# ScalarE takes shared results, row numbers and the slot map; TensorE's maps and shared chunks stand in another order; one gather goes in front of scatters

## The reference, cut to what matters

```python
x = L0_attn_x                                    # 8 x 512 tokens, 256 wide
x = layernorm(x + attn(x))                       # gated attention, two layernorms of its own
# the mixture of experts, on all 4096 tokens:
shared = gelu(xf @ Wfc_s + bfc_s) @ Wproj_s + bproj_s          # 256 -> 1024 -> 256
probs  = softmax(xf @ Wr);  topk_p, topk_i = top_k(probs, 2)   # 2 of 8 experts
topk_p = topk_p / sum(topk_p)
for e in range(8):
    h = gelu(xf @ Wfc[e] + bfc[e]) @ Wproj[e] + bproj[e]
    routed = routed + h * gate[:, e:e + 1]       # gate is 0 for experts not chosen
x = layernorm(x + shared + routed)
```

## Time and profile before

| | |
|---|---|
| median of 3 runs | 1000.14 us (999.05 to 1000.84) |
| the profiled execution: time / span | 1000.27 us / 998.4 us |
| PE busy | 936.1 us (94% of the span) |
| DVE busy | 752.9 us (75%) |
| ACT busy | 566.6 us (57%) |
| POOL busy | 234.3 us (23%) |
| mean granted clock of PE | 0.979 |
| chain that ended last | PE 57%, DVE 6%, ACT 1%, DMA 1%, issue 1% (shares below 1% left out) |

### The profile page before, as it was taken

The page is one execution under the profiler, slowest core; times in us unless marked ns, Lnnn a source line. Parts: engine busy times, 40 slices in busy tenths (PEclk is TensorE's granted clock), DMA queues, the critical chain, the costliest instruction groups (busy, mean ns, idle before and its releaser), DMA issues.

```text
span 998.4 us, 17975 instructions
## 1 busy us (share of the span) xinstructions
PE 936.1 (94%) x5998; PEld 830.3 (83%) x5998; DVE 752.9 (75%) x1823; ACT 566.6 (57%) x1008; POOL 234.3 (23%) x170
## 2 busy tenths in 40 slices
PE   4979999999997988899999999999999989999995
PEld 3767788788876777799999999999999989999994
DVE  5799889888876589677777777777777879984846
ACT  5625556655645532355555555555555768874654
POOL 0050000000000000324444444444444444421000
PEclk9979999999999998999999999999999999999998
DMA  4130323231333422245555555555555678877302
GB/s 155 58 117 30 129 69 126 68 127 52 106 114 126 145 44 85 72 130 127 133 138 132 141 155 147 132 134 135 136 143 143 177 194 226 237 223 222 106 22 85
DMA packets 66869, 125.88 MB, mean 126 GB/s; under 512 B 13629, under 2 KB 52384, under 8 KB 60289
## 3 DMA queue, kind: packets, MB, share of 16 engines
q1 hardware_dynamic: 48144, 101.02, 30.4%
q0 software_dynamic: 14976, 20.54, 12.4%
q10 hardware_dynamic: 3696, 3.67, 1.1%
HBM read 92.40 MB, written 31.75 MB: 124 GB/s over the span
## 4 chain that ended last, share of the span: by engine, by line
PE 57%; DVE 6%; ACT 1%; DMA 1%; issue 1%; POOL 0%; DVEq 0%
PE bank L1460 28%; PE bank L1503 27%; PE bank L1488 2%; DVE s_hl L1382 1%; DVE s_acc L1256 1%; DMA s_xb<-x_rows,s_token 1%; DVE s_until_map L1258 1%; DVE s_until_map L1257 1%; DVE s_acc L1344 0%; POOL residual_sums L1080 0%; ACT s_hh L1130 0%; PE bank L1457 0%; ACT s_h L1126 0%; DVE s_until_map L1259 0%; PE bank L1523 0%
## 5 line engine op out<-in xcount | busy, mean ns | idle before, releaser
L1126 ACT ACTIVATE s_h<-bank,k_bfc 128x512 f32<-128x512 f32 (+1 forms) x248 | 154.6, 623 | 248.0 <-PE bank L1503 236.2
L1382 DVE TENSOR_TENSOR s_hl<-s_h,s_hh 128x512 fp32r<-128x512 f32 (+1 forms) x248 | 151.8, 613 | 144.0 <-ACT s_hh L1130 142.9
L1080 POOL DMA_INDIRECT residual_sums<-s_y,s_dest x78 | 132.8, 1703 | 233.0 <-DVE s_y L1330 216.6
L1071 POOL DMA_INDIRECT s_xb<-x_rows,s_token x78 | 84.8, 1087 | 382.3 <-DVE s_dest L1272 342.3
L1130 ACT ACTIVATE s_hh<-s_h 128x512 fp32r<-128x512 f32 (+1 forms) x248 | 141.4, 570 | 11.4 <-ACT s_h L1126 1.4
L1503 PE MATMUL bank<-k_uh,k_wfc1h 128*128 128x512 f32 (+1 forms) x448 | 139.6, 361 | 0.5 <-PEq L191 0.5
L1460 PE MATMUL bank<-s_wpj0l,s_hh 128*128 128x256 f32 x448 | 126.0, 281 | 1.4 <-DVE s_hl L1382 1.4
L1460 PE MATMUL bank<-s_wpj0h,s_hh 128*128 128x256 f32 x448 | 126.0, 281 | 0.0
L1460 PE MATMUL bank<-s_wpj0h,s_hl 128*128 128x256 f32 x448 | 125.8, 281 | 0.0
L1460 PE MATMUL bank<-k_wpj1l,s_hh 128*128 128x256 f32 x400 | 113.2, 283 | 0.2 <-DVE s_hl L1382 0.2
L1460 PE MATMUL bank<-k_wpj1h,s_hh 128*128 128x256 f32 x400 | 113.1, 283 | 0.0
(11 more groups left out here) (297 smaller groups left out, 2159.2 us busy)
## 6 DMA issues: line engine op xcount, KB each, us to landing
k_wstage<-wall SPq DMA_DIRECT2D x50, 1024.0 KB, 5.6
s_x_in<-x SPq DMA_DIRECT2D x8, 512.0 KB, 4.2
s_x_res<-x SPq DMA_DIRECT2D x8, 512.0 KB, 4.7
x_rows<-s_x SPq DMA_DIRECT2D x8, 512.0 KB, 3.5
residual_sums<-s_x SPq DMA_DIRECT2D x8, 512.0 KB, 4.2
x_parts<-s_x1h SPq DMA_DIRECT2D x8, 512.0 KB, 2.6
x_parts<-s_x1l SPq DMA_DIRECT2D x8, 512.0 KB, 3.7
k_uh<-x_parts SPq DMA_DIRECT2D x8, 512.0 KB, 4.9
```

The source lines that it names most:

```text
L1071: pool.indirect_dma_start(xb[i][:, t, :], None, X1D, bass.IndirectOffsetOnAxis(token[:, at:at + 1].bitcast(U32), 0), bounds_check=N - 1).t ...
L1080: pool.indirect_dma_start(RES, bass.IndirectOffsetOnAxis(dest[:, at:at + 1].bitcast(U32), 0), y[:, t, :], None, bounds_check=N + S - 1, co ...
L1126: nc.scalar.activation(h[j % 2][:, cols], b[:, cols], ACT.Gelu_apprx_tanh, bias=bfc[w][:, j:j + 1]).then_inc(h_ev, 1)
L1382: tt(hl[j % RING][:, cols], h[j % 2][:, cols], hh[j % RING][:, cols].bitcast(F32), ALU.subtract).then_inc(hl_rd, 1)
```

## The change

1. Attention, steps B and B+1. VectorE takes `hl` of chunk 0 between the moments and the reciprocal root of the second norm, chunk 1 behind it, and the remainder `x1l` before it writes `z`; chunks 2 and 3 follow between and behind the two `z` passes. TensorE and ScalarE take chunks 2 and 3 ahead of the logits, chunk 6 ahead of the transposes of `x1`, chunk 7 and `proj(6)` behind them, so that only `proj(7)` is left for step B+2.
2. ScalarE, not VectorE, copies the results of shared blocks 0 to 3 out of PSUM, right after the rounded copy of chunk 1 of the next block.
3. ScalarE, not VectorE, multiplies the row one-hots by the row number (in place, 16-bit, once per group), and copies the slot map out of PSUM; VectorE reads that copy. TensorE's `proj` of n = 3, j = 0 waits for the copy and no longer for `token` and `dest`.
4. TensorE multiplies group g one chunk later than before, and the counts one chunk later (behind `fc(5)` of n = 1).
5. On GpSimd gather(17) is issued in front of scatter(14) and not behind it.

```diff
# ScalarE, attention
-                if at(B + 2):
-                    beside(7)
...
+                if at(B + 1):
+                    beside(6)
                 if last:
...
                 if at(B):
-                    beside(2)
+                    beside(2, 3)
                 if at(B + 1):
-                    beside(6)
+                    beside(7)
...
                 if at(B):
-                    beside(3, 4, 5)
+                    beside(4, 5)
# VectorE, attention, second norm
-                    rstd(TT, 2 * TT)
+                    now = slice(TT, 2 * TT)
+                    moments(nc, link, st[:, now, :], mean[:, now], var[:, now], tmp[:, now])
+                    if at(B):
+                        beside(0)
+                    rsqrt(nc, link, rs[:, now], half[:, now], var[:, now], tmp[:, now])
+                    if at(B):
+                        beside(1)
+                        x1_rest()
                     for t in range(TT):
                         stt(z[:, t, :], yo[t], mean[:, TT + t:TT + t + 1], ln2[:, 0, :], ALU.subtract, ALU.mult).then_inc(o_ev, 1)
+                    if at(B):
+                        beside(2)
...
+                if at(B):
+                    beside(3)
# TensorE, attention
                 if at(B + 2):
-                    fc(KH - 1)
+                    proj(KH - 1)
...
                 if at(B):
-                    beside(2)
+                    beside(2, 3)
                 if at(B + 1):
-                    beside(6)
+                    beside(7)
+                    proj(KH - 2)
# GpSimd
             for r in range(ROUTED):
+                if r == BIG - 1:
+                    gather(r + 3, side(r + 3))
                 scatter(r, side(r))
-                if r + 3 < ROUTED:
+                if r != BIG - 1 and r + 3 < ROUTED:
                     gather(r + 3, side(r + 3))
# ScalarE, experts
+            def shared_result(n, i):
+                act.wait_ge(pj_mm, (n + 1) * KH)
+                for t in range(ST):
+                    nc.scalar.activation(acc[:, n * ST + t, :], yb[i][t // 2][:, t % 2 * D:t % 2 * D + D], ACT.Copy).then_inc(acc_rd, 1)
+            def row_numbers(g):
+                act.wait_ge(hot_rd, g + 1)
+                rows = codes[:, g * HOT:(g + 1) * HOT, COLS:]
+                nc.scalar.activation(rows, rows, ACT.Copy, scale=cst[:, ROW_NO:ROW_NO + 1]).then_inc(row_rd, 1)
+            def slot_map_out():
+                act.wait_ge(map_mm, 1)
+                nc.scalar.activation(slot_map[:, :], bank[6][:, 0:2 * COLS], ACT.Copy).then_inc(map_ev, 1)
+            dispatch = {**{(2, g + 1): lambda g=g: row_numbers(g) for g in range(KH - 1)}, (3, 0): lambda: row_numbers(KH - 1),
+                        (3, 1): slot_map_out}
...
+                    if j == 1 and is_int(n) and n <= FIRST:
+                        shared_result(n - 1, 1 - i)
+                    if is_int(n) and (n, j) in dispatch:
+                        dispatch[n, j]()
# VectorE, experts
-                link(tt(signed, row, each(cst[:, CODE:CODE + 2 * NT][:, at], COLS), ALU.mult))
-                ts(row, row, cst[:, ROW_NO:ROW_NO + 1], None, ALU.mult).then_inc(hot_rd, 1)
+                tt(signed, row, each(cst[:, CODE:CODE + 2 * NT][:, at], COLS), ALU.mult).then_inc(hot_rd, 1)
...
-                dve.wait_ge(map_mm, 1)
-                signed, row = bank[6][:, 0:COLS], bank[6][:, COLS:2 * COLS]
+                dve.wait_ge(map_ev, 1)
+                signed, row = slot_map[:, 0:COLS], slot_map[:, COLS:2 * COLS]
# TensorE, experts
                     if is_int(n) and n == 3:
-                        pe.wait_ge(map_rd, 1)
+                        pe.wait_ge(map_ev, 1)
...
-            map_after = {(2, 2): (0, 1), (3, 0): (KH - 1,), **{(2, j): (j - 1,) for j in range(3, KH)}}
+            map_after = {(3, 0): (KH - 2,), (3, 1): (KH - 1,), **{(2, j): (j - 2,) for j in range(2, KH)}}
...
                         for g in map_after[n, j]:
                             pe.wait_ge(hot_rd, g + 1)
+                            pe.wait_ge(row_rd, g + 1)
```

More of the change, by code:

```diff
@@ L550, in step, with x1_rest @@
                     stats([x_in[:, t, :] for t in range(TT)], 0)
-                if at(B + 1):
-                    beside(3)
                 if ahead or last:
                     need(dve, xn_ready, min(b, B - 1) + 1 if is_int(b) else b + 1)
-                    rstd(0 if ahead else TT, 2 * TT if last else TT)
-                    shifts(0 if ahead else TT, 2 * TT if last else TT)
-                if at(B + 1):
-                    beside(4)
+                    now = slice(0 if ahead else TT, 2 * TT if last else TT)
+                    moments(nc, link, st[:, now, :], mean[:, now], var[:, now], tmp[:, now])
+                    if at(B + 1):
+                        beside(4)
+                    rsqrt(nc, link, rs[:, now], half[:, now], var[:, now], tmp[:, now])
+                    shifts(now.start, now.stop)
                 if at(B + 1):
                     beside(5)
+                def x1_rest():
+                    for k in range(KD):
+                        dve.wait_ge(x1h_rd, 2 * c + k + 1)
+                        tt(x1l[:, k, :], x1T[:, k, :], x1h[:, k, :].bitcast(F32), ALU.subtract).then_inc(x1l_rd, 1)
                 if main:
@@ L606, in step @@
                     xT_rest(b + 1)
-                def x1_rest():
-                    for k in range(KD):
-                        dve.wait_ge(x1h_rd, 2 * c + k + 1)
-                        tt(x1l[:, k, :], x1T[:, k, :], x1h[:, k, :].bitcast(F32), ALU.subtract).then_inc(x1l_rd, 1)
                 def rest(m):
@@ L625, in step @@
                     rest(KE - 1)
-                elif last:
-                    if at(B):
-                        beside(0, 1)
+                elif at(B + 1):
+                    beside(6)
                     x1_rest()
-                    beside(*((2,) if at(B) else (6, 7)))
+                    beside(7)
             dve.wait_ge(ld_x, 16)
@@ L846, in step @@
                 if at(B):
-                    beside(3, 4, 5)
-                if at(B + 2):
-                    for j in (5, 6, 7):
-                        proj(j)
+                    beside(4, 5)
             pe.wait_ge(ld_v0, 32)
@@ L1321, in _ @@
                       (1, 4): counts, (1, 5): starts, (1, 6): slots_in_blocks, (1, 7): slots, (2, 0): lambda: (one_hots(0), owners()),
-                      **{(2, j): lambda j=j: one_hots(j) for j in range(1, KH)}, (3, 1): slot_map}
+                      **{(2, j): lambda j=j: one_hots(j) for j in range(1, KH)}, (3, 1): slots_of_blocks}
             def y_results(r, i, small=False):
@@ L1335, in shared_result @@
                 dve.wait_ge(pj_mm, (n + 1) * KH)
-                if late(n):
-                    dve.wait_ge(ld_y[n - ROUTED], 16)
+                dve.wait_ge(ld_y[n - ROUTED], 16)
                 for t in range(ST):
-                    tok = acc[:, bass.ds((n - ROUTED if late(n) else n) * ST + t, 1), :].rearrange("p o d -> p (o d)")
+                    tok = acc[:, (n - ROUTED) * ST + t, :]
                     shared_y = yb[i][t // 2][:, t % 2 * D:t % 2 * D + D]
-                    if late(n):
-                        tt(tok, shared_y, tok, ALU.add).then_inc(acc_rd, 1)
-                    else:
-                        nc.vector.tensor_copy(tok, shared_y).then_inc(acc_rd, 1)
+                    tt(tok, shared_y, tok, ALU.add).then_inc(acc_rd, 1)
             def total(piece, batch_rows):
@@ L1384, in tokens @@
                         beside[n, j]()
-                    if j == 1 and (r is None or (is_int(r) and r == 0)) and not (is_int(n) and n in (0, LATE[0])):
+                    if j == 1 and late(n) and n > LATE[0]:
                         shared_result(n - 1, 1 - i)
@@ L1505, in tokens @@
                     last.then_inc(fc_mm, 1)
-                    if is_int(n) and n == 1 and j == 4:
+                    if is_int(n) and n == 1 and j == 5:
                         pe.wait_ge(both_rd, 1)
```

8 lines of the change are left out of this document (5 added, 3 removed).

## The result

The changed kernel takes 973.96 us (median of four runs, 972.62 to 976.62) against 999.96 beside it, a ratio of 0.9748 with a 95% interval of 0.9732 to 0.9763. The forecast was 970.6 us and a range of 966.5 to 977.0: the time lies in the range, 3.4 us above the forecast. The profiled execution took 973.68 us with a span of 971.9, so 26.5 us went out of the span where 29.6 were forecast.

The account below looks back on a forecast made before the run. TensorE was taken as the bound, losing time to waits, mostly for VectorE, and a slow clock. Savings 9.5 + 2.9 + 10.0 + 1.5 + 5.7 = 29.6 us off a 998.4 us span gave 970.6 us, range 966.5 to 977.

Parts of the forecast that it names:

- End of attention, 9.5: Steps B and B+1: both TensorE waits and the slow clock behind them go, saving 9.5 us.
- margins of 0.3 us: End of attention: inputs for the logits and the transposes are ready only 0.3 us before TensorE needs them.
- Block n = 1, 2.9: Block n = 1: the 2.1 us wait and slow clock go, some idle and two short waits remain; saves 2.9 us.
- 1.65 of clock: Block n = 1: work lost to a clock of 0.95 over 33 us, expected back: 1.65 us.
- Block n = 2 and the map, 10.0: Block n = 2 and map: 14.2 us of idle and clock go, less 4.2 of new waits; saves 10.0 us.
- slope of 0.82 ns: ScalarE's row multiply: time per column between 256 and 512 columns, used to put the multiply at 0.80 us.
- Behind the map, +1.5: From the map to T of block 0: of 1.7 us lost to the clock, 1.5 us are kept.
- equal within 0.2: First gather: 10.5 us until its release against TensorE's 10.3 us of work, so the 3 us slack is gone.
- first gather becomes the bound: Rival behind the map: the gather lands 4.0 us later, TensorE waits 4 and loses 1.7 to the clock; 976.3, chance 0.13.
- Switch, 5.7: Switch to small blocks: the gather lands before TensorE wants it, so idle 4.07 and clock 1.67 go; saves 5.7 us.
- TensorE is never short: Steady run of small blocks: with a gather behind only two scatter DMAs, TensorE never lacks work.
- 1 to 1.7 us for a fallen clock: Block n = 2 and map: should the clock fall behind the new short waits, it costs 1 to 1.7 us.

Follow-up runs that it names:

- both edits: Changed kernel with ScalarE copying the slot map before block 2's results and expert 1's weight load held until the first gather lands: 970.39 us, ratio 0.9707.
- row numbers twice: Changed kernel with ScalarE copying the same rows in place once more behind each row multiply, values unchanged: 974.73 us, ratio 0.9744.
- edit 4: As a run: changed kernel with only the later order undone, so TensorE multiplies each map group and the counts one chunk earlier: 985.63 us, ratio 0.9888.
- edit 1 back: Changed kernel with only the reordering at the end of attention undone, attention written as before: 983.69 us, ratio 0.9845.
- row multiply back: Changed kernel with only the multiply of the row one-hots returned from ScalarE to VectorE: 976.08 us, ratio 0.9763.
- edit 5: As a run: changed kernel with only the gather's move undone, scatter(14) again ahead of gather(17): 980.23 us, ratio 0.9813.
- row numbers thrice: Changed kernel with ScalarE copying the same rows in place two more times behind each row multiply: 976.24 us, ratio 0.9764.
- edit 2: As a run: changed kernel with VectorE again copying the results of shared blocks 0 to 3 out of PSUM: 976.35 us, ratio 0.9778.
- multiply and edit 4 back: Changed kernel with the row multiply on VectorE and the old order of map groups and counts, both: 980.30 us, ratio 0.9802.

## Why the prediction was right, and where it was not

- *End of attention, 9.5.* Right: 9.4 by the landmarks, 9.9 when undone. The margins of 0.3 us held in the changed kernel, but they are as thin as I said: in the run with both edits TensorE waits 0.3 for `z` (L688 <- DVE s_z L594) and the piece is 0.4 longer, and with the row numbers twice it waits 0.2 and the piece is 0.3 longer. Neither edit touches attention.
- *Block n = 1, 2.9.* Right: 3.1, of which the copies alone are 1.3 and the counts' later place 0.4; what is left, 1.4, is near the 1.65 of clock in the sum. The kernel before has 0.95 there, and each of the two runs with one half undone has 1.00, so in these traces the clock was lost only where both delays met.
- *Block n = 2 and the map, 10.0.* Right in size and cause: ScalarE's multiply at 0.80 (0.81 measured), VectorE's chunk 3.30 (3.30), TensorE's 3.4 (3.42), new waits 4.2 (3.3). ScalarE: Activation LUTs, in the Trainium skill ("What ACT_TABLE_LOAD costs") gives 280 ns and 0.833 ns an element for an operation with an operand per partition, 0.80 for 624, and the trace agrees. The rule of the same page in the Trainium skill ("Rules for kernel authors"), that a multiply belongs on VectorE, fits the instruction (0.38 against 0.81) and not this kernel in the new order, and fits the kernel in the old order: the 2 x 2 of multiply and order shows both. What the prediction did not see is how much hangs on edit 4. It gave the order no price of its own; the order alone is 10.5. Undone one by one, edits 2, 3 (the multiply) and 4 cost 2.8, 2.3 and 10.5, more than the 10.2 of all together, so these prices don't add. The map's copy on ScalarE, with the shorter wait of `proj`, was not undone in any run. And the slope of 0.82 ns behind the 0.80 is not in the earlier trace rows as shown: it is that of the rounded copy, 0.633 us at 512 columns and 0.418 at 256.
- *Behind the map, +1.5.* Wrong: -0.5. The failed step is "GpSimd starts 1.0 later, and its first four gathers take 7.96 from 412.45 to the release at 420.41: 10.5 us", with "equal within 0.2" drawn from it. The 1.0 held and the issues nearly (4.56 for 4.35); the landing did not: the fifth issue came 6.35 us behind the fourth and not 3.6. I carried a DMA's duration over from a trace in which its neighbour was elsewhere. SyncE's load is paced by TensorE's chunks (VectorE's split of expert 0's weights releases it) and the gather by `dest`; before, the wait of `proj` for `dest` tied the two together, and the change cut exactly that tie. This is read from the rows, where the load goes out 7.6 us behind the first gather's first issue before and 4.6 after; no run puts the tie back. "Equal within 0.2" was wrong in a second way: 10.5 is the time to GpSimd's fifth issue, and TensorE is released some 0.7 earlier (401.87 against 402.52). So there was a slack of about 0.8, and 2.7 of landing became a wait of 1.9. Without that wait the piece would have gained 1.4, so the term itself was well sized. The rival "first gather becomes the bound" named the place and its mechanism and priced it at 4.0 of landing and 1.7 of clock; it came with 2.7 of landing, 1.9 of wait and no fall of the clock.
- *Switch, 5.7.* Right: 5.7 by the landmarks, 6.0 when undone.
- *The rest, 0.* The trace had -0.9, and -0.5 at the start. Neither is the change's: twelve further traces scatter by more. "TensorE is never short" in the small blocks is too strong: it waits 0.2 for `hl` there.
- The sum misses by 3.1 us of span: 2.0 are the first gather, 1.4 those two pieces, and the other terms are 0.3 better than forecast.

## What to carry to other kernels

Before a duration of a DMA is carried over to a changed kernel, list what else will be in flight then, by what releases each transfer: where a wait is removed, the two sides of it can be paced by different engines from then on. A product that waits for another engine's work on the chunk just issued makes a ring; its length is the sum of what stands in it. Here one chunk of distance in the order was worth 10.5 us, and moving the multiply from one engine to the other 2.3. Waits of one engine behind another need not add: here the first absorbed the one after it. Before a growth is put down to waits, look at the clock of the stretch: here it made 1.7 of 2.7 us in one run, and nearly all of 2.8 in another.

## What the runs showed of the hardware

- The issue that waits for a gather of four indirect DMAs comes 3.62 us behind the gather's last issue with no load beside it (3.61 in the kernel before, 3.65 with both edits). When a weight load of 1024 KB on another queue starts 0.03 to 0.04 us behind that last issue, it comes 6.1 to 7.2 us behind in nine traces; 0.9 us of lead bring it to 4.59.
- The clock behind a single wait of 1.7 to 2.8 us for the first gather went either way. With a wait of 2.8 (edit 1 back) it stayed at 1.00 over the 10 us behind, and so it did with 1.9, 2.2 and 2.4 (the changed kernel twice, row multiply back) and with 1.7, 1.8, 2.0 and 2.1 (edit 4, edit 5, row numbers thrice, edit 2). With 2.5 (row numbers twice) it was 0.84 over 10.5 us, which makes most of the +2.1 of that run, and with 2.1 (multiply and edit 4 back) 0.82 over 9.5. Edit 1 back, row numbers twice, and multiply and edit 4 back:

```profile
412.60:422.60 10.00, 9.98 (x65) 9.11 (x66) 5.55 (x12) 5.04 (x8) 4.40 (x5) 1.00 0.26 65
```

```profile
403.50:414.00 10.50, 10.32 (x58) 9.28 (x59) 4.99 (x11) 4.45 (x7) 4.08 (x4) 0.84 0.19 52
```

```profile
408.50:418.00 9.50, 9.50 (x53) 8.44 (x52) 4.44 (x8) 3.72 (x6) 4.09 (x4) 0.82 0.21 57
```

What decides it stays open: the length of the wait alone does not. The prediction's 1 to 1.7 us for a fallen clock behind a short wait has the right size here (0.16 x 10.5 and 0.18 x 9.5 are both 1.7), and its place is the range and not the sum.
